# Normalisation moved from VectorE to GpSimd and ScalarE in a four-layer attention kernel, with one operation less per cross head and new orders

## The reference

```python
def L0(x, ctx):            # L3s: self attention with a mask; L3c: like L0 plus a mask
    h = layer_norm(x) ; q, k, v = h @ q_w + q_b, ctx @ k_w + k_b, ctx @ v_w + v_b
    x = x + attention(q, k, v, heads=16) @ cproj_w + cproj_b
    return x + gelu(layer_norm(x) @ fc_w + fc_b) @ proj_w + proj_b
def L1(x, ctx):            # keys and values from ctx and x together (256 keys)
    a = attention(x @ q_w, [ctx; x] @ kv_w) @ out_w + out_b + x
    return gelu(rms_norm(a) @ w1 + b1) @ w2 + b2 + x
def L2(x, ctx):            # twice cross attention: 16 heads of width 128, one more key/value from bias_k, bias_v
    for j in (1, 2): x = x + cross_attention(layer_norm(x), ctx)
    return x + gelu(layer_norm(x) @ w_fc1 + b_fc1) @ w_fc2 + b_fc2
x = L3(L2(L1(L0(x, ctx), ctx), ctx), ctx)
```

## Time and profile before

| what | us |
|---|---|
| median of 3 runs | 1100.99 (1098.34 to 1101.16) |
| profiled execution, its own time | 1098.16 |
| its span, first to last instruction | 1096.9 |
| PE busy | 1051.5 |
| DVE busy | 780.4 |
| ACT busy | 576.7 |
| POOL busy | 537.0 |

### The profile page before, as it was taken

One profiled execution on the slowest core, in us unless ns is written; L12 is line 12 of the kernel. 1 busy time (PEld: TensorE's weight loads), 2 busy tenths in 40 slices (PEclk: granted clock), 3 DMA queues, 4 the chain that ended last, 5 costly groups with the idle time before them and its releaser, 6 DMA issues.

```text
span 1096.9 us, 20208 instructions
## 1 busy us (share of the span) xinstructions
PE 1051.5 (96%) x7794; PEld 921.7 (84%) x7794; DVE 780.4 (71%) x1217; ACT 576.7 (53%) x1250; POOL 537.0 (49%) x547
## 2 busy tenths in 40 slices
PE   6999999999999999999998999999999999987898
PEld 4778887888888999999986999999998878766787
DVE  6988788889545766766567666765665588999871
ACT  4988787778433223222242323333233678878682
POOL 2644344444643443443375433443523388887860
PEclk9999999999999999999999999999999999999999
DMA  8200000000112222212130011110000000000000
GB/s 337 104 1 21 1 1 2 1 1 2 48 59 77 78 68 68 72 35 68 39 100 14 27 39 40 39 39 22 28 1 1 1 1 1 1 1 1 11 10 20
DMA packets 33782, 40.65 MB, mean 37 GB/s; under 512 B 2111, under 2 KB 31257, under 8 KB 32025
## 3 DMA queue, kind: packets, MB, share of 16 engines
q1 hardware_dynamic: 33689, 39.38, 10.9%
HBM read 38.32 MB, written 1.05 MB: 36 GB/s over the span
## 4 chain that ended last, share of the span: by engine, by line
PE 71%; DVE 13%; issue 5%; POOL 5%; ACT 5%; DMA 0%; SPq 0%; POOLq 0%; DVEq 0%; ACTq 0%
PE psum L640 14%; PE psum L467 12%; PE psum L534 8%; PE psum L699 7%; PE psum L654 7%; PE psum L687 4%; PE psum L668 4%; PE psum L560 4%; PE psum L550 2%; ACT C tile L1165 2%; PE psum L575 2%; PE psum L677 2%; PE psum L518 2%; DVE C xn L826 2%; DVE C sum L873 1%
## 5 line engine op out<-in xcount | busy, mean ns | idle before, releaser
L1382 POOL TENSOR_TENSOR B tile<-B tile,B rec 128x1024 f32<-128x1024 f32 x32 | 60.7, 1897 | 212.3 <-DVE B rec L986 212.3
L1307 POOL TENSOR_TENSOR A tile<-A tile,A rec 128x1024 f32<-128x1024 f32 x48 | 90.8, 1903 | 123.3 <-DVE A rec L875 123.3
L1209 ACT ACTIVATE B own<-B max 128x8 f32<-128x8 f32 x32 | 6.7, 210 | 194.3 <-DVE B tile L974 194.3
L1165 ACT ACTIVATE A tile<-A tile,A min 128x128 f32<-128x128 f32 (+1 forms) x256 | 91.4, 449 | 6.1 <-DVE A min L868 5.9
L1165 ACT ACTIVATE C tile<-C tile,C min 128x128 f32<-128x128 f32 x256 | 77.6, 392 | 11.8 <-DVE C min L868 11.8
L1111 ACT ACTIVATE B kT<-psum,B bcol 128x1024 f32<-128x1024 f32 x32 | 35.7, 1116 | 88.9 <-PE psum L640 88.9
L1014 DVE TENSOR_TENSOR x_all<-x_all,psum 128x512 f32<-128x512 f32 x64 | 42.5, 684 | 55.2 <-PE psum L699 55.2
L467 PE MATMUL psum<-C hT,weights 128*128 128x256 f32 x352 | 81.6, 385 | 0.2 <-ACT C hT L1111 0.2
L467 PE MATMUL psum<-A hT,weights 128*128 128x256 f32 x352 | 81.4, 384 | 0.1
L467 PEld LDWEIGHTS psum<-C hT,weights 128*128 128x128 f32 x352 | 66.4, 192 | 11.0 <-ACT C hT L1111 1.0
L654 PE MATMUL psum<-B v hi,B cT hi 128*128 128x256 f32 x256 | 74.6, 291 | 1.0 <-DVE x_all L1014 1.0
(11 more groups left out here) (198 smaller groups left out, 3139.7 us busy)
## 6 DMA issues: line engine op xcount, KB each, us to landing
weights<-in_weights_c SPq DMA_DIRECT2D x6, 1024.0 KB, 6.2
raw<-in_wq SPq DMA_DIRECT2D x32, 128.0 KB, 2.5
raw<-in_wk SPq DMA_DIRECT2D x32, 128.0 KB, 2.9
raw<-in_wv SPq DMA_DIRECT2D x16, 256.0 KB, 2.5
raw<-in_wo SPq DMA_DIRECT2D x16, 256.0 KB, 2.8
weights<-in_weights_a SPq DMA_DIRECT2D x1, 3072.0 KB, 21.2
weights<-in_weights_a SPq DMA_DIRECT2D x1, 2048.0 KB, 11.5
wide<-in_bias_v SPq DMA_DIRECT2D x2, 1024.0 KB, 4.5
```

The costliest lines, as they stand in the source:

```text
L1165: i = act.activation(of_head, of_head, ACT.Exp, bias=part.min[:, u % 4, h:h + 1], scale=-1.0)
L1307: pool.tensor_tensor(tile(u, ly.nk), tile(u, ly.nk), part.rec[:, u % 4, 0:ly.per].unsqueeze(2).to_broadcast([P, ly.per, ly.nk]), ALU.mult) ...
L1382: pool.tensor_tensor(tv, tv, m.brec[:, h, :].unsqueeze(2).to_broadcast([P, B, S]), ALU.mult).then_inc(s["normalised"].sem, s["normalised"] ...
```

## The change

1. The normalisations leave DVE. Those of L0 and those before the MLP of L1 go to POOL, all others to ACT: `XN_ON`, and always ACT for `out`. ACT computes rstd * x + nb, so POOL makes nb = -mean * rstd for each in one more one-column instruction (`shift`), except for the root-mean-square form. Between the cross halves too (`next_xn` on ACT, two shifts a block on POOL).
2. In the second outer stage ACT drains the heads (`HEADS_ON`).
3. ACT's list opens with one exponential on a small tile, which loads the table; the waits for columns and parity move to the first drain that reads them. DVE makes the parity biases after `stats L0 in 0 1`.
4. A cross head loses the clamp of its maxima. The subtraction is max(m, 0) - s in one instruction, and the exponential takes scale -1; the own key's exp is capped at 1 as it is added.
5. The small tiles of the outer stages are shared, the value weights' cut waits for the end of the first stage's weighing itself, and both orders are new. Each holds the same steps as before, 437 and 330.

The diff, cut to its core (of the orders only the beginning of the first is shown):

```diff
+XN_ON = {"L0": "POOL", "L1": "POOL", "M2": "ACT", "L3s": "ACT", "L3c": "ACT"}
+HEADS_ON = {"A": "DVE", "C": "ACT"}
 ORDER_ONE = """
-    stats L0 in 0 0, ctx 0 1, stats L0 in 0 1, xn L0 in 0 0, xn L0 in 0 1, stats L0 in 1 0, stats L0 in 1 1, turn_in L0 in 0 0, xn L0 in 1 0, k L0 0 0 2,
-    stats L0 in 2 0, q L0 0 1, xn L0 in 1 1, ctx 2 7, xn L0 in 2 0, stats L0 in 3 0, scores 0, minima 0, turn_in L0 in 1 5, ctx 1 7, exp 0 0, exp 0 1,
+    stats L0 in 0 0, ctx 0 7, k L0 0 0 7, xn L0 in 0 0, stats L0 in 0 1, xn L0 in 0 1, stats L0 in 1 0, v L0 0 0 2, turn_in L0 in 0 5, stats L0 in 1 1,
+    stats L0 in 2 0, stats L0 in 3 0, stats L0 in 2 1, ctx 2 4, xn L0 in 2 0, q L0 0 0, xn L0 in 2 1, stats L0 in 3 1, ctx 1 7, scores 0, ctx 3 7,
...
 # vector_program
-        def normalise(name, of, k, b):
-                i = dve.tensor_scalar(part.xn[k][:, b, :], m.x(k)[:, b, :], part.mv[k][:, b, 0:1], rstd, ALU.subtract, ALU.mult)
+                if a == ("L0", "in", 0, SB - 1):
+                    parities()
-            elif what == "weigh" and units[a[0]][2:] in ENDS:
+            elif what == "weigh" and units[a[0]][2:] in ENDS and HEADS_ON[st] == "DVE":
-        dve.tensor_scalar(mx, mx, 0.0, None, ALU.max).then_inc(s["max_made"].sem, s["max_made"].mark(event))
-        dve.tensor_tensor(tv, sc, mx.unsqueeze(2).to_broadcast([P, B, S]), ALU.subtract).then_inc(s["bshifted"].sem, s["bshifted"].mark(event))
+        dve.scalar_tensor_tensor(out=tv, in0=mx.unsqueeze(2).to_broadcast([P, B, S]), scalar=0.0, in1=sc, op0=ALU.max, op1=ALU.subtract).then_inc(
-        dve.tensor_tensor(total, total, m.own[:, h, :], ALU.add).then_inc(s["total_made"].sem, s["total_made"].mark(event))
+        dve.scalar_tensor_tensor(out=total, in0=m.own[:, h, :], scalar=1.0, in1=total, op0=ALU.min, op1=ALU.add).then_inc(s["total_made"].sem, s["total_made"].mark(event))
 # scalar_program
+        def normalise(name, of, k, b):
+            event, rstd = (name, of, k, b), part.rstd[k][:, b:b + 1]
+            if (name, of) == ("L1", "mlp"):
+                act.wait_ge(s["rstd_made"].sem, s["rstd_made"].at(event))
+                i = affine(part.xn[k][:, b, :], part.xb[k][:, b, :], rstd, None)
+            else:
+                act.wait_ge(s["nb_made"].sem, s["nb_made"].at(event))
+                i = affine(part.xn[k][:, b, :], m.x(k)[:, b, :], rstd, part.nb[k][:, b:b + 1])
+            i.then_inc(s["xn_act"].sem, s["xn_act"].mark(event))
-    act.wait_ge(s["cols_made"].sem, s["cols_made"].at("cols"))
-    act.wait_ge(s["parity_made"].sem, s["parity_made"].at("biases"))
+    act.wait_ge(s["pool_done"].sem, s["pool_done"].at("half"))
+    act.activation(m.warm[:, :], m.half[:, :], ACT.Exp)
+            next_xn(0)
+            next_xn(1)
             for n in range(NS):
                 features(("N", n), m.nh[n], ("L2_ln2_scale", "L2_ln2_offset"))
                 upper_part(2, n, ("N", n), m.nh[n])
+                if n < 2:
+                    next_xn(n + 2)
 # gpsimd_program
+    def shift(event, mean, rstd, nb, b):
+        pool.tensor_scalar(nb[:, b:b + 1], mean, rstd[:, b:b + 1], -1.0, ALU.mult, ALU.mult).then_inc(s["nb_made"].sem, s["nb_made"].mark(event))
+        def normalise(name, of, k, b):
+                i = pool.tensor_scalar(part.xn[k][:, b, :], m.x(k)[:, b, :], part.mv[k][:, b, 0:1], rstd, ALU.subtract, ALU.mult)
```

More of the change, by code:

```diff
@@ L51, with xn_on, xn_signal @@
 PIECE = WEIGHT_COLS // (NP_ - 2)
+def xn_on(name, of):
+    return "ACT" if of == "out" else XN_ON[name]
+def xn_signal(name, of):
+    return "xn_act" if xn_on(name, of) == "ACT" else "xn_pool"
 def earlier(of, things, n=1):
@@ new lines @@
+    exp 22 1, scores 23, residual L1 mlp 2, even 22 1, weigh 21, minima 23, turn_in L1 mlp 2 7, turn 22 0, exp 23 0, down L1 1 1 0, even 23 0,
+    project 21 3, exp 23 1, stats L1 out 1 0, even 23 1, turn 22 1, up L1 2 0 7, up L1 2 2 1, weigh 22, turn 23 0, stats L1 out 0 1, up L1 2 4 0,
+    turn 23 1, stats L1 mlp 3 0, up L1 2 6 3, xn L1 mlp 3 0, weigh 23, ctx_parts 0, value_weights, ctx_parts 1, down L1 2 0 3, xn L1 out 0 0,
+    weights_of 0, project 23 4, stats L1 mlp 3 1, xn L1 out 0 1, down L1 2 1 7, turn_in L1 out 0 5, xn L1 mlp 3 1, xn L1 out 1 0, turn_in L1 mlp 3 7,
@@ L896, in do @@
                 stats(*a)
-            elif what == "xn":
-                normalise(*a)
+                if a == ("L0", "in", 0, SB - 1):
+                    parities()
             elif what == "q":
@@ L1107, in scalar_program, with once @@
     act, bank = nc.scalar, m.bank
-    zeroed = set()
+    known = set()
+    def once(signal, event):
+        if (signal, event) not in known:
+            known.add((signal, event))
+            act.wait_ge(s[signal].sem, s[signal].at(event))
     def affine(dst, src, scale, bias):
@@ L1136, in values @@
             event = (name, "v", k, src)
-            if st not in zeroed:
-                zeroed.add(st)
-                act.wait_ge(s["zeros_set"].sem, s["zeros_set"].at(st))
+            once("zeros_set", st)
             act.wait_ge(s["v_projected"].sem, s["v_projected"].at(event))
@@ L1182, in do @@
                 exponential(*a)
+            elif what == "xn" and xn_on(*a[:2]) == "ACT":
+                normalise(*a)
+            elif what == "weigh" and units[a[0]][2:] in ENDS and HEADS_ON[st] == "ACT":
+                heads(*a)
             elif what == "ctx_parts":
@@ L1317, in do @@
                 rstd(tuple(a), part.ve[a[2]][:, a[3]:a[3] + 1], part.rstd[a[2]][:, a[3]:a[3] + 1], 1)
+            elif what == "xn" and xn_on(*a[:2]) == "POOL":
+                normalise(*a)
+            elif what == "xn" and tuple(a[:2]) != ("L1", "mlp"):
+                _, _, k, b = a
+                pool.wait_ge(s["rstd_made"].sem, s["rstd_made"].at(tuple(a)))
+                shift(tuple(a), part.mv[k][:, b, 0:1], part.rstd[k], part.nb[k], b)
             elif what == "residual":
@@ L1386, in next_rstd @@
         rstd(("N", k), m.nve[k][:, :], m.nrstd[k][:, :], SB)
+        pool.wait_ge(s["rstd_made"].sem, s["rstd_made"].at(("N", k)))
+        for b in range(SB):
+            shift(("N", k, b), m.nmv[k][:, b, 0:1], m.nrstd[k], m.nnb[k], b)
     def lower_part(j, k, h):
```

212 lines of the change are left out of this document (110 added, 102 removed).

## The result

| kernel | median us | runs | ratio |
|---|---|---|---|
| before | 1099.81 | 4, 1098.34 to 1101.16 | |
| changed | 1088.36 | 4, 1085.43 to 1092.67 | 0.990, 95% interval 0.9871 to 0.9928 |

The change makes the kernel faster by 11.4 us, 1.0%, with an interval clear of 1; 1087 was forecast. The profiled execution of the changed kernel is the slowest of the four, 1092.67 us with a span of 1091.4, and its mean granted clock is 0.991; two of the four had 1.000 and took 1085.4 and 1085.7. The kernel before had 0.997 at best in its runs near these times. In what follows a "fall" is a short stretch in which TensorE's granted clock goes to the lower of its two levels; how many falls a run has changes its time by several us, so stages are compared at the same number of falls.

What follows compares the result with a forecast made beforehand. PE, busy 96% of the span, bounds the kernel, so only its 45.4 us of idle time can be won. Terms 3.5 + 1 - 0.5 + 3 + 7 = 14 us, off the median 1100.99, gave 1087; range 1075 to 1103.

Steps and rivals of the forecast that it cites:

- The second outer stage, forecast 7 us: Second outer stage, 860 to 1070 us: unloading DVE shrinks PE's idle 17.5 us; gain 7, ends -5 and 14.
- One of its signs of being wrong: Prediction is wrong if ACT's idle time shows long waits for POOL's shift.
- the point of decision: Slower rival, second outer stage: decides once ACT's busy and waiting exceed 210 us by 7: 35 us, 1.7 a piece.
- The entry of that stage, forecast -0.5: Second outer stage's entry: the exposed input normalisation becomes three links instead of two; -0.5 us, ends -1.5 and 0.
- I cost it at 0: Cross halves: removing 32 clamps, 24.5 us of DVE time, gains 0 because PE is full there.
- the term for the entries: Cross stage entry: last normalisation leaves DVE's queue, one clamp goes per opening head; gain 1 us, ends -1 and 2.
- together 3.5: First stage's start: 0.5 us net before 20 us, 3 from unloading DVE between 20 and 70; ends 0 and 8.
- I take 0.55: First stage: price in us of each of 24 POOL normalisations, bracketed by 0.40 and 0.74; 13 us in all, hidden.
- Another sign of being wrong: Prediction is wrong if PE now idles in the middle of the first stage where it did not.
- Between the halves, forecast 3: Between cross halves: ACT takes eight normalisations, ending its row at 581.3, DVE's at 582.1, against 585.15; ends 0 and 4.
- ACT takes DVE's place: Rival, second outer stage: 860 to 1070 gains nothing as ACT waits like DVE did; 1094 us, chance 0.17.
- That ACT waits for POOL's shift: Slower rival, second outer stage: 21 ACT normalisations wait behind POOL's long operations; 1116 us at 2.4 a piece, chance 0.13.

Runs made afterwards that it cites:

- the run with a clock of 1.000: The changed kernel without the exponential that opens ScalarE's list, its waits kept as changed: 1088.52 us, 0.9884 of the kernel before.
- the placement with the old orders: The changed kernel with both orders of before, keeping the moved normalisations, head drains, clamp and table: 1173.68 us, 1.065 of before.

## Why the prediction was right, and which of its steps were not

**What bounds.** Right: PE's busy time did not change, the gain came from its idle time, and the largest part from the second outer stage.

**The sum at equal clock.** The forecast was 14 us, the medians differ by 11.4, and runs of the two kernels with the same mean clock differ by 8.5 (0.995: 1097.6 and 1097.8 against 1089.1 and 1089.5) to 9.5 us (0.994: 1100.4 to 1100.8 against 1091.0 to 1091.2; all of one group). The profiles give 8.4 to 9.1 at the same number of falls: first stage 0.9 to 1.6 longer (325.5 before, 326.4 to 327.1 after, one fall each), first half 0.8 shorter, between the halves up to 0.9, second half 0.8, second outer stage 7.5 (267.1 and 259.6, one fall each). So that the medians came so near to 1087 is in part luck: some 2 us of the measured gain are the clock, for which no term stood, and two terms of 3 and 3.5 us brought next to nothing.

**The second outer stage, forecast 7 us.** Right: the stretch went from 210 to 204 us, with one fall before and two after. DVE 150.4 (forecast 145), ACT 178.4 (182), POOL 166.1 (167.5), PE idle 11.3 (10). Of what is left of the idle time 6.1 us is PE's wait for POOL's multiplication, as the prediction had it. The table loads came out as counted, 26 against 28: two more in the first stage, four less in the second. The price of a shift was mis-sized, 0.33 for 0.2, and the normalisation on ACT 0.60 for 0.5. The experiments split the gain into 7.6 us for the normalisations and 3.7 for the heads, each against the new orders with that part back on DVE; with both back that stage is longer than before, 269.8 us against 267.1. What the prediction read as the price of the stage, 1.285 us for a normalisation on DVE, was a price of the old order (0.60 to 0.64 with the new). One of its signs of being wrong did show: ACT waits for POOL's shift, nine times, 12.6 us in all, up to 4.4 us. It did not decide the stage, since it stays under the 35 us of the point of decision.

**The entry of that stage, forecast -0.5.** Outside the stretch the stage went from 57.1 us to 56.8, a gain of 0.3 where the ends were -1.5 and 0; the stage's end is in this figure too, and it was not taken apart.

**The cross halves and the entry of the first.** "I cost it at 0", with the two opening turns left to the term for the entries, was the right place: all that the clamp gives lies in the opening turns, 0.8 us each. The entry of the cross stage was forecast at 1; the opening of the first half is 0.8 of it. What the normalisation that leaves DVE's queue there brings lies in the first stage's milestone and was not measured by itself. The second half's opening had no price of its own. These lengths repeat to 0.1 us, so they are the surest of the measured terms. The remaining 1.5 us of the first half's 2.3 lie in the clock: before's profile has 0.67 in the slice of 5 us that begins at 335, the changed one has none in that half.

**The start, "together 3.5".** The step that failed. The beginning was right: no load behind a wait, the context is drained at 5.87 us, key matmuls begin at 7.27, and the scores start at 17.98 (16.86 in the run without the exponential) against 16.68, later as foreseen. But PE's idle time from 20 to 70 us is 5.9, not 1 (4.2 before), and in the whole stage it is 13.6 us before, 14.0 after and 13.9 in the run with a clock of 1.000. No idle time went. DVE fell only from 48.9 to 45.3 busy us from 20 to 70, where 7 us less were forecast. PE's largest wait there, before and after:

```profile
PE psum L550 <- DVE A tile L861: 3.1, 2, 2.2
PE psum L574 <- POOL A tile L1357: 2.8, 2, 2.5
```

The size of a POOL normalisation, "I take 0.55", was wrong (1.25), and POOL's busy time from 20 to 70 rose from 24.3 to 29.3. But the trace does not make this the cause. The two multiplications that PE waits for (it goes on at 29.53 and 33.09) find POOL idle, and what released them is DVE's reciprocal:

```profile
27.57 1.90 POOL L1357 TENSOR_TENSOR A tile<-A tile,outer rec 128x1024 f32<-128x1024 f32 x1 [1.63 <-DVE outer rec L879]
31.14 1.90 POOL L1357 TENSOR_TENSOR A tile<-A tile,outer rec 128x1024 f32<-128x1024 f32 x1 [1.67 <-DVE outer rec L879]
```

And with the normalisations back on DVE the stage is 3 us longer at equal clock. So the chain of the first softmaxes through DVE still sets the pace after the change; it starts 0.2 to 1.3 us later, with values now in front of the scores. That the work taken from DVE would give PE's idle time back was the wrong link. How much of this is the order and how much DVE's remaining work was not taken apart. Another sign of being wrong showed weakly: from 70 to 300 us PE idles 1.1 us, where it was 0.15.

One reading in this paragraph of the prediction needs a note: the granted clock before 20 us is 1.00 in the earlier trace rows, so the profile's column does not show "the lower clock level" there. What it shows is that eight key matmuls take 3.43 us from 6.83 on in the run without the exponential, and eight of the same shape 1.99 us at 14.86 in the changed kernel.

**Between the halves, forecast 3.** The second term that failed: at most 0.9. The stretch is 24.0 us before and 23.2 (clock 1.00), 24.6 and 26.0 after. ACT does the normalisations in the row foreseen, with an idle time before them of 4.3 us on POOL's shifts, but then PE's last waits there are for the lower parts of the features (2.4 us for POOL's, 1.9 for DVE's), which nothing had made faster. What was priced was an ACT row without the wait for POOL. Its working is off too: four blocks of 2.6 us from 569.7 end at 580.1, not 581.3.

**The clock.** No term stood for it. The runs of each kernel fall into steps that follow the mean granted clock, as the last section shows. Steps of the clock are as large as single terms of the forecast, so that medians cannot settle terms of 1 to 3 us; stages at the same number of falls can, as far as single profiles go.

**The rivals.** That ACT takes DVE's place did not happen: with the normalisations on ACT the stage is 7.6 us shorter, though in the first stage the same move costs 4 to 5 us in all. The Trainium skill, "ScalarE: Activation LUTs", section "Rules for kernel authors", with its advice to multiply and add on VectorE, is borne out in the first outer stage (1096.00 us on ACT, 1091.42 on DVE) and not in the second (1091.05 on ACT, 1097.86 on DVE); the runs at hand decide it by place. That ACT waits for POOL's shift was given 0.13; it is the truth of the placement with the old orders, at 17 waits and 69.5 us, and of the changed kernel at 9 waits and 12.6 us. The point of decision, 35 us of waits, lies between the two.

## What to carry to other kernels

A move of work between engines that run in order and the order itself are one change: judge neither by a run of it alone, since each here was a loss and only both a gain. The price of an operation read from one order need not hold in another: DVE's normalisation was 1.01 us in the old order of the second outer stage and 0.60 in the new. When a step gets a producer on another engine, look for what is queued ahead of the producer's small instruction, and put work between the two in the order. The price of an operation on GpSimd is not to be had from a row of another form (0.40 for a cast and 0.74 for a subtraction bracketed 0.55; it was 1.25), and it pays to look at which waits come first in an engine's list, since they also hold what would need none of them.

## What the runs showed that I had not expected

**The same kernel, two clocks.** The slice from 30 to 40 us, in the changed kernel and in the one without the first exponential (length, busy times, granted clock):

```profile
30.00:35.00 5.00, 2.53 (x15) 2.29 (x14) 3.19 (x6) 5.00 (x18) 3.52 (x2) 0.73 0.92 316
35.00:40.00 5.00, 5.00 (x58) 3.58 (x57) 3.42 (x4) 1.98 (x5) 3.60 (x4) 0.59 0.04 15
```
```profile
30.00:35.00 5.00, 2.60 (x28) 2.01 (x28) 3.09 (x5) 5.00 (x16) 3.79 (x2) 1.00 0.92 311
35.00:40.00 5.00, 4.60 (x69) 3.71 (x69) 4.96 (x8) 4.07 (x10) 4.36 (x3) 1.00 0.00 0
```

PE was idle alike, about 2.4 us of the first five, in both. In one run the clock fell within this to the lower of its two levels (0.59, nearer to 1.2 than to 2.4 GHz), and 58 matmuls took all 5 us; in the other it stayed, and 69 took 4.60. In the profiles of the changed kernel this happens at up to four places, near 32, 580, 978 and 998 us, and costs about 2 to 3 us in the first stage, 1.5 to 3 between the halves, and 0.7 and 2.0 for one and for two falls in the last stage. So the runs of one kernel differ by 8 to 10 us in steps: for the kernel without the exponential 1084.7 at 1.000, 1085.7 and 1086.4 at 0.998, 1090.7 at 0.994, 1092.5 at 0.991; for the kernel before 1095.8 to 1096.4 at 0.997, 1103.7 to 1106.0 at 0.989 and 0.990. A difference of 3 us between two medians can be one or two such steps. What decides whether it falls behind the same pause was not found.

**A load needs no instruction of its own.** The table load ran at 0.78 us in a kernel whose first activation came at 6.02: it did not wait for the data of its activation. In the kernel before, with two waits ahead of it in the list, it ran at 6.35.

**Prices.** GpSimd's subtraction and multiplication by two columns on 128x256 takes 1.25 us, the multiplication by one column 0.93, and the same with two operations on a tile of a single column (128x1) 0.33. On ACT the form with scale and bias from memory is 0.60 us wherever it stood. On DVE one and the same form and shape took from 0.36 to 2.54 us in the second outer stage of the kernel before, and had a mean of 1.01 there and 0.60 to 0.64 with the new orders. What lengthens single ones was not looked at.
